# A perceiver layer's cross-attention: GpSimd subtracts the maxima without first waiting for the running maximum of the preceding tile

## The reference

```
q = rms_norm(layernorm(x) @ Wq); k = rms_norm(ctx @ Wk); v = ctx @ Wv     # 16 heads of 64
scores = where(row < len[b], q.k / 8, NEG_INF)
x = x + (softmax(scores) @ v) @ Wo
x = x + sparse_attention(layernorm(x));  x = x + quantized_ffn(layernorm(x))
```

## Time and profile before

| | |
|---|---|
| median of 3 runs | 2843.41 us (2842.18 to 2843.88) |
| the profiled execution | 2840.21 us, its span 2838.4 us |
| mean granted TensorE clock | 0.955 of full speed |
| busy over the span | PE 2520.1 us (89%), PE weight loads 2152.0, DVE 2048.0 (72%), ACT 1396.7 (49%), POOL 1121.0 (39%) |
| `shift` (L562) | 416 operations, 985.5 us busy, 2373 ns each, 1271.4 us idle before them |
| `keep_best` (L703) with two different inputs | 352 operations, 432.2 us busy, 1228 ns each |
| one batch element in the loop | 63.5 us: POOL's runs of two operations (steps 0 and 1) start at 439.98 and, 12 batch elements on, at 1202.42 |

### The profile page before, as it was taken

How to read it: one execution, slowest core, us unless ns; L and a number is a source line. 1 busy time by engine, 2 the same in 40 slices (tenths; PEclk the granted TensorE clock), 3 DMA queues, 4 the chain that set the end, 5 groups by cost and what they waited for, 6 DMA issues and landing times. The chain is left out here.

```text
span 2838.4 us, 54155 instructions
## 1 busy us (share of the span) xinstructions
PE 2520.1 (89%) x16440; PEld 2152.0 (76%) x16440; DVE 2048.0 (72%) x3024; ACT 1396.7 (49%) x3025; POOL 1121.0 (39%) x542
## 2 busy tenths in 40 slices
PE   4565899999999999999999999999999968699842
PEld 2453688888888888888888888888888857577622
DVE  4444988888888888888888888888888801566567
ACT  4443355555555555555555555555555431366530
POOL 0000145444444444544444444544444550122235
PEclk9778999999999999999999999999999989899975
DMA  0463111111111111111111111111111017000000
GB/s 30 178 242 109 55 48 47 46 46 61 47 46 59 47 55 47 45 47 61 47 53 52 54 47 46 46 59 49 46 59 47 27 57 248 16 0 0 0 0 15
DMA packets 144247, 162.13 MB, mean 57 GB/s; under 512 B 10513, under 2 KB 117969, under 8 KB 144081
## 3 DMA queue, kind: packets, MB, share of 16 engines
q1 hardware_dynamic: 139600, 144.86, 15.6%
q10 hardware_dynamic: 4608, 16.78, 1.4%
HBM read 110.22 MB, written 51.38 MB: 57 GB/s over the span
## 5 line engine op out<-in xcount | busy, mean ns | idle before, releaser
L562 POOL TENSOR_TENSOR probs<-scores,best_all 128x1024 f32 (+2 forms) x416 | 985.5, 2373 | 1271.4 <-DVE best L703 1263.9
L816 PEld LDWEIGHTS u_ps<-rows,probs 128*128 128x128 f32 x6656 | 806.1, 192 | 53.4 <-issue 9.2
L688 DVE SCALAR_TENSOR_TENSOR scores<-s_ps,mask,rrms 128x512 f32 (+2 forms) x832 | 619.8, 746 | 304.1 <-PE s_ps L761 303.7
L816 PE MATMUL u_ps<-rows,probs 128*128 (+1 forms) x6656 | 811.0, 275 | 13.4 <-ACT probs L635 11.0
L635 ACT ACTIVATE probs<-probs 128x1024 f32<-128x1024 f32 (+1 forms) x416 | 439.4, 1057 | 427.0 <-POOL probs L562 427.0
L596 ACT ACTIVATE squares<-k_ps 128x512 f32<-128x512 f32 (+1 forms) x832 | 471.4, 598 | 234.5 <-PE k_ps L761 151.2
L667 DVE TENSOR_REDUCE ssq<-squares 128x16 f32<-128x1024 f32 (+1 forms) x416 | 502.7, 1208 | 0.0
L703 DVE TENSOR_TENSOR best<-best,scores 128x1024 f32<-128x1024 f32 (+1 forms) x352 | 432.2, 1228 | 0.3
L759 PE MATMUL k_ps<-w_hi,cT_hi 128*128 128x512 f32 (+1 forms) x832 | 363.8, 437 | 23.2 <-DVE cT_lo L661 23.2
L759 PE MATMUL s_ps<-q_hi,cT_hi 128*128 (+2 forms) x832 | 361.9, 435 | 3.5 <-ACT uT_sb L616 1.4
L761 PE MATMUL k_ps<-w_hi,cT_lo 128*128 128x512 f32 (+1 forms) x832 | 328.5, 395 | 0.0
(11 more groups left out here) (197 smaller groups left out, 2488.3 us busy)
## 6 DMA issues: line engine op xcount, KB each, us to landing
stage<-in_ctx SPq DMA_DIRECT2D x384, 64.0 KB, 1.8
rows<-in_ctx SPq DMA_DIRECT2D x32, 768.0 KB
queries_hi<-p_hi SPq DMA_DIRECT2D x16, 1024.0 KB, 4.1
queries_lo<-p_lo SPq DMA_DIRECT2D x16, 1024.0 KB, 6.2
q_hi<-queries_hi SPq DMA_DIRECT2D x32, 512.0 KB, 3.7
q_lo<-queries_lo SPq DMA_DIRECT2D x32, 512.0 KB, 4.4
u_transposed<-uT_sb ACTq DMA_DIRECT2D x32, 512.0 KB, 3.0
a_uT<-u_transposed SPq DMA_DIRECT2D x16, 1024.0 KB, 4.8
```

What stands on the lines that cost most here:

```text
L562: pool.tensor_tensor(probs[0:r, slot_of(c, PRING), :], scores_at(b, c), best_all[0:r, bass.ds((b % 2) * HL, HL)], ALU.subtract).then_inc(s ...
L688: dve.scalar_tensor_tensor(out=scores_at(p, c, h * HALF, HALF).rearrange("p (h l) -> p h l", l=L), in0=s_ps[h][0:r, :].rearrange("p (h l) ...
L816: last = pe.matmul(u_ps[g // 3][:, at:at + UW], probs[0:r, s, g * P:(g + 1) * P], rows, start=(c == 0 and g % 3 == 0), stop=(c == NC - 1), ...
```

## The change

The two waits are taken out of POOL's step. Nothing else is changed: POOL's other waits (L560, L561), the order of each queue, and all other engines' work stay.

```diff
             def step(p, c, on):
                 n = p * NC + c
                 if on.shift:
-                    if c > 1 and on.scores:
-                        pool.wait_ge(kept.sem, kept.ended(p, c - 1))
-                    if c == 0 and on.rows:
-                        pool.wait_ge(kept.sem, kept.ended(p - 1))
                     shift(p - 1 if c + 1 >= LAG else p - 2, n + 1 - NC - LAG, (c + 1 - LAG) % NC)
```

## The result

The changed kernel takes 2954.74 us (median of 4 runs, 2953.93 to 2959.17) against 2842.8 us: 1.0401 times the time of before, 95% interval 1.0383 to 1.0419. That is slower by 112 us, where 170 (3013 us) was forecast: the sign and about two thirds of the size.

The account below looks back on a forecast made before the run. PE was taken to bound the kernel. Per batch element 1.2 + 2.1 + 1.2 + 0.95 + 0.3 = 5.75 us, for 30 of them 170 us; profiled 2840.2 + 170 = 3010, median 3013 us, range 2878 to 3040.

Parts of the forecast that it names:

- rival A: DVE gets its turn between two POOL operations; 1.5 us per batch element, 45 us, 2888 us (2870 to 2910); chance 0.20.
- Where the subtractions go: POOL's subtractions start 2.10 us after PE's value run begins; three in a row from step 4, two in step 2.
- A caught operation ends 1.09 us after POOL: At the SBUF port: a `keep_best` caught by a POOL subtraction ends 1.09 us after POOL does.
- Step 12 to 0: Between batch elements: POOL catches the first Newton operation, `keep_best` and PE come late; 1.2 us per batch element.
- Who gets in between two POOL operations in a row: In rows of two or three subtractions, `keep_best` waits for the last; based on DVE's 7791 ns in the FFN.
- Step 5: `keep_best` waits for POOL's row of three subtractions, 6.98 us, and PE is late by 1.2 us per batch element.
- step 6: DVE, 2.17 us late, delays reciprocals, divisions and the split PE waits for; 0.95 us more per batch element.
- Step 2: `keep_best` waits for POOL's subtractions of tiles 11 and 12; PE is late by 2.1 us per batch element.
- Steps 7 to 11: One subtraction per step catches `keep_best`; PE is late only once, by 0.3 us per batch element.
- B: Subtractions run ahead and DVE's slack swallows the blocking; 2843 us, no change; chance 0.08 together with D.
- C: POOL enters the last part with a lead, so ACT and PE wait less there; 2835 us, faster; chance 0.06.
- D: The slot wait ends later than `keep_best` did, so POOL isn't freed; time as in B, chance counted there.

Follow-up runs that it names:

- e1: The changed kernel with the wait of step 0 put back: 2919.81 us, 1.0273 times the kernel before.
- e2: The kernel before with only the wait of step 0 taken out: 2843.26 us, 1.0007 times the kernel before.
- e3: The changed kernel with `mean_squares` as a `tensor_reduce`, 1/64 moved into ACT's squares, EPS left out: 2894.28 us, 1.0183 times the kernel before.
- e6: The kernel before with a satisfied wait in front of each of POOL's 12 FFN operations on `f_gate`: 2830.99 us in a single run.
- e7: The kernel before with POOL's 12 FFN operations on `f_gate` as `tensor_tensor` with two SBUF inputs, a sum instead of the rounding: 2843.59 us.
- e9: The changed kernel with the wait of step 0 put back and `mean_squares` as a reduce, EPS left out: 2857.01 us, 1.0049 times the kernel before.
- e8: The kernel before with the wait taken out in step 5 alone: 2838.43 us, 0.9988 times the kernel before.
- e10: The kernel before with the wait out in step 5 alone and satisfied waits before POOL's 12 FFN operations on `f_gate`: 2832.94 us, 0.9969.

## Why the prediction was right and where it was wrong

The direction held, and the mechanism in its main part: POOL, no longer held back, catches operations of DVE, and DVE's lateness reaches PE. One step of it failed, and the time is right with some luck. 2954.74 lies in the wide range, 2878 to 3040, but between the forecast's own 2990 to 3035 and the 2870 to 2910 of rival A: no scenario of the prediction gives it. Of its signs, the longer `keep_best` (1756 ns) and L69 (1.45 us) came true. The longest `keep_best` is that of rival A (3.39 us, not near 5). The period of 67.08 lies between 65 and 69.3. PE waits for `cT_lo` 0.9 us per batch element instead of some 5, and its longer wait is for `best_row`, not for the split, which the prediction itself gave as a sign of being wrong. Taken by its own steps:

- *PE sets the pace, ACT's and POOL's waits are worth nothing.* Right: POOL no longer waits for DVE, ACT's wait for POOL is down to 22.4 us over the span, and nothing was gained.
- *Where the subtractions go.* Right: POOL's releaser is PE's value run, the runs of two and three lie in steps 2 and 4 to 5.
- *A caught operation ends 1.09 us after POOL.* Right: 3391 ns at most, 3.45 forecast for one POOL operation.
- *Step 12 to 0, 1.2 us.* Measured 1.16; e1 takes it away.
- *Who gets in between two POOL operations in a row.* Wrong, and this is the step that failed. From the earlier trace rows I took `keep_best` to wait for the last of a row. It waits for the operation in progress; POOL's next is held instead (3.32 us in step 5, 3.41 in e2, 3.31 in e3, where 2.36 is its own time). The Trainium skill has it so in "SBUF — State Buffer", section "Who interferes with whom": the second to issue is blocked until the first has finished. For the subtractions the trace agrees. For the FFN's 7.8 us it does not, and e6 and e7 show that to be a special case of that code. I had named the difference, "the shifts have satisfied ones", and given it too little weight.
- *Step 5, 1.2 us, and step 6, 0.95.* Both 0, by the same failure. These 2.15 us per batch element, 65 in all, cover the 58 by which the forecast was too high (170 against 112).
- *Step 2, 2.1 us.* Measured 1.60 + 0.27 = 1.87, nearly the forecast, but by luck: the forecast had `keep_best` held to the end of a row of two, and that did not happen. `mean_squares`, which was not in the argument, turned one block into two. e3 removes it and with it the loss.
- *Steps 7 to 11, 0.3 us.* Measured 0.24 (1238.01 to 1239.95 instead of 1.70) and 0.13 in the next step.
- *30 equal batch elements and -5 to +5 at the end.* Nearly: 7.1 for the first, twice the others, 3.0 at the end.

Together 5.75 were forecast per batch element, and 3.54 measured. Rival A had the right arbitration and the wrong sum: 1.5 us, 2888 us, for want of `mean_squares`. Its 1.5 plus the 60 / 30 = 2.0 us of e3 make 3.5. B and C fell: DVE's slack took up the caught `keep_best`, as B says and e9 shows, but not the small operations in front of those on which PE waits. D fell with the timeline.

## What to carry to other kernels

A wait that looks needless may keep two engines off a shared resource; before it is taken out, list every instruction that would then lie beside the other engine's work, the 0.2 us ones too, and ask of each what stands behind it in its queue. In this kernel 194 us of holding in DVE's slack are left in e9, which is 14 us slower than before; holding three small operations per batch element (two `mean_squares`, one of Newton's) in front of what PE waits for cost 98. A hold seen in one stage is evidence for another only if the instructions, and the waits between them, are of the same kind.

## What the runs showed of the hardware that was not expected

- A DVE `tensor_scalar` with one SBUF input of 64 or 144 columns is held by a POOL `tensor_tensor` just as an operation with two inputs: 2.25 us instead of 0.2. A `tensor_reduce` with one SBUF input never was (64 columns 0.22 us, 1024 columns 1.22 us at most in 352). The Trainium skill, "SBUF — State Buffer", section "Who interferes with whom", counts `tensor_scalar` among the operations that can contend with GpSimd, and says of `tensor_reduce` that it never does on trn2; the runs agree. The price here comes from the queue behind the operation, not from its length.
- A row of POOL `tensor_scalar` operations without waits between them held a DVE operation for 7.8 us, over ten ends of operations. A satisfied wait in front of each, or two SBUF inputs, ended that (1.1 and 1.7 us). With the wait the kernel is faster: by 5.5 us from e8 to e10, whose intervals barely overlap.
